# A two-layer transformer block on one core: the last batch's projection first, another batch's down product in TensorE's pause

## The reference

```python
x = layernorm(x + attn0(x))        # 16 heads of 8, softmax over all 256 keys
x = layernorm(x + ffn0(x))         # 128 -> 512, butterflies, gelu, butterflies, 512 -> 128
x = layernorm(x + attn1(x))        # low-rank q and kv, RoPE, causal softmax
x = layernorm(x + ffn1(x))         # silu(x @ wg.T) * (x @ wu.T) @ wd.T, hidden size 384
```

## Time and profile before

| | |
|---|---|
| median of 3 runs | 326.21 us |
| the three runs | 324.72, 326.21, 326.78 us |
| the profiled execution | 325.87 us |
| its span | 324.1 us |
| mean granted TensorE clock | 0.959 |
| busy share of the span: PE, DVE, ACT, POOL | 85%, 78%, 67%, 63% |

### The profile page before, as it was taken

The page is one execution under the profiler, slowest core; times in us unless marked ns, Lnnn a source line. Parts: engine busy times, 40 slices in busy tenths (PEclk is TensorE's granted clock), DMA queues, the critical chain, the costliest instruction groups (busy, mean ns, idle before and its releaser), DMA issues.

```text
span 324.1 us, 9463 instructions
## 1 busy us (share of the span) xinstructions
PE 275.0 (85%) x3194; PEld 200.0 (62%) x3194; DVE 253.7 (78%) x991; ACT 216.5 (67%) x444; POOL 205.3 (63%) x326
## 2 busy tenths in 40 slices
PE   8989969988978999888998896988898787878763
PEld 4766646655565556554676565866676666667553
DVE  4778796886878778897676697598999999775555
ACT  2546883788976799499983999468685757444110
POOL 0529995472448546584779897498879747366332
PEclk9979997999999999999995999899999999899978
DMA  7784350303021130404013140401314040000000
GB/s 228 258 254 144 93 192 15 131 1 131 3 97 35 32 133 17 150 4 155 8 46 120 23 145 11 153 1 41 126 35 148 3 148 20 2 2 18 17 16 32
DMA packets 20495, 25.84 MB, mean 80 GB/s; under 512 B 3744, under 2 KB 14304, under 8 KB 20320
## 3 DMA queue, kind: packets, MB, share of 16 engines
q1 hardware_dynamic: 20016, 24.72, 22.9%
q10 hardware_dynamic: 432, 0.53, 0.4%
HBM read 6.36 MB, written 1.05 MB: 23 GB/s over the span
## 4 chain that ended last, share of the span: by engine, by line
PE 51%; DVE 25%; issue 12%; ACT 9%; POOL 2%; POOLq 0%; ACTq 0%; DVEq 0%
PE bank L632 14%; DVE mx L864 6%; PE bank L388 5%; PE bank L647 4%; DVE room_c L872 4%; ACT E L760 4%; PE bank L398 4%; PE bank L576 4%; PE bank L515 2%; PE bank L597 2%; DVE room_c L898 2%; PE bank L407 2%; PE bank L586 2%; DVE turned L954 2%; PE bank L608 2%
## 5 line engine op out<-in xcount | busy, mean ns | idle before, releaser
L760 ACT ACTIVATE E<-bank 128x512 f32<-128x512 f32 (+1 forms) x256 | 119.7, 549 | 65.4 <-PE bank L411 37.9
L864 DVE TENSOR_REDUCE mx<-bank 128x2 f32<-128x512 f32 x128 | 79.6, 681 | 13.0 <-PE bank L388 12.8
L872 DVE CUSTOM_DVE_ANT_0 room_c<-bank,mask_sb 128x256 f32<-128x256 f32 (+1 forms) x256 | 72.9, 349 | 2.3 <-PE bank L388 2.1
L388 PE MATMUL bank<-QK 32*128 32x256 f32 x480 | 56.0, 308 | 8.4 <-DVE mx L872 3.4
L398 PE MATMUL bank<-QK 32*128 32x256 f32 x480 | 51.8, 311 | 11.5 <-DVE hid L900 6.7
L632 PE MATMUL bank<-E,V 128*32 128x256 f32 (+1 forms) x1024 | 59.5, 376 | 0.2
L388 PEld LDWEIGHTS bank<-QK 32*128 32x128 f32 x480 | 38.4, 187 | 21.4 <-issue 8.9
L1083 POOL TENSOR_SCALAR_AFFINE_SELECT E<-E 128x512 f32<-128x512 f32 x64 | 39.2, 638 | 11.6 <-ACT E L760 11.6
L398 PEld LDWEIGHTS bank<-QK 32*128 32x128 f32 x480 | 35.1, 188 | 17.5 <-DVE hid L900 9.0
L632 PEld LDWEIGHTS bank<-E,V 128*32 128x32 f32 x1024 | 31.0, 115 | 20.7 <-issue 3.6
L954 DVE STREAM_TRANSPOSE turned<-bank 128x256 f32<-128x256 f32 x32 | 14.3, 447 | 21.2 <-PE bank L632 20.9
(11 more groups left out here) (127 smaller groups left out, 561.7 us busy)
## 6 DMA issues: line engine op xcount, KB each, us to landing
spread_qk<-parts SPq DMA_DIRECT2D x30, 256.0 KB, 2.5
spread_qk<-parts SPq DMA_DIRECT2D x60, 128.0 KB, 2.2
room_c<-room_c SPq DMA_DIRECT2D x64, 32.0 KB, 1.9
xb<-x_nat SPq DMA_DIRECT2D x1, 1024.0 KB, 7.1
out<-ln_g SPq DMA_DIRECT2D x7, 128.0 KB, 1.9
xt<-x_t SPq DMA_DIRECT2D x1, 768.0 KB, 7.1
wi<-wi_all SPq DMA_DIRECT2D x1, 576.0 KB, 3.5
room_c<-fac_u SPq DMA_DIRECT2D x1, 508.0 KB, 6.4
```

The lines of the kernel that those rows point to most:

```text
L388: ins = nc.tensor.matmul(g_bank["max", m][:, cols], both[:, 0, c * P:(c + 1) * P], both[:, 1, keys], start=True, stop=True)
L760: act.activation(E[:, a % E_RING, j, 0:n], g_bank["exp", m][:, 0:n], ACT.Exp, scale=SCALE)\
L864: ins = nc.vector.tensor_reduce(mx[:, n % 2, :, i], bank[:, :].rearrange("p (q k) -> p q k", q=QT), AX.X, ALU.max, negate=True)
L872: ins = nc.vector.tensor_tensor_reduce(out=masked_s[:, at % 2, lo:hi], in0=bank[:, lo:hi], in1=mask_sb[:, T + lo - hi:T], scale=-1.0, scal ...
```

## The change

Two entries of `FFN1` move: the down product of batch 13 with its residual and statistics goes from step 264 to 268 (its scaling stays at 272), and the third up chunk of batch 14 from 268 to 264, which moves its tanh too, but not its gate. In TensorE's loop the bodies of transposes and output projection become functions, and for batch 15 alone they are called at another place: the projection ahead of the up chunks of its step, the transposes behind the down product of theirs.

```diff
--- before.py
+++ after.py
@@ -50,8 +50,8 @@
 AT_UP0, AT_GELU, AT_DN0, AT_LN0, AT_XT0 = (52, 52, 56, 56), 60, (64, 68), 72, 76
 
 FFN1 = {b: ((40, 40, 48), 64, 68) for b in range(NB, BATCHES)}
-FFN1.update({BATCHES - 4: ((40, 40, 52), 60, 64), BATCHES - 3: ((40, 44, 52), 56, 64),
-             BATCHES - 2: ((36, 40, 44), 52, 56), BATCHES - 1: ((32, 32, 32), 40, 44)})
+FFN1.update({BATCHES - 4: ((40, 40, 52), 60, 64), BATCHES - 3: ((40, 44, 52), 60, 64),
+             BATCHES - 2: ((36, 40, 40), 52, 56), BATCHES - 1: ((32, 32, 32), 40, 44)})
 
 LATE_GATES = {(BATCHES - 3, 2): HEADS + 4, (BATCHES - 2, 0): HEADS + 8, (BATCHES - 2, 1): HEADS + 12, (BATCHES - 2, 2): HEADS + 12}
 
@@ -524,6 +524,26 @@
                                            wv_sb[:, :] if layer(b) == 0 else wl1[:, 2, :], start=True, stop=True)
                 ins.then_inc(A["v_ps"], 1)
 
+            def turn_tokens(b, g):
+
+                bank = claim(("xt", b), A["xt_ready"], b + 1, g)
+                pe.wait_ge(A["ln_ready"], b + 1)
+                for q in range(QT):
+                    ins = nc.tensor.transpose(bank[:, q * P:(q + 1) * P], NA["ln"][:, b % LN_RING, q, :], id32[:, :])
+                ins.then_inc(A["xt_ps"], 1)
+
+            def project_out(b, g):
+                bank = claim(("proj", b), A["res_done"], b + 1, g)
+                pe.wait_ge(A["att_ready"], b + 1)
+                if b == 0:
+                    pe.wait_ge(ld["bv"], 32)
+                elif b == NB:
+                    pe.wait_ge(ld["next"], 64)
+                for q in range(QT):
+                    ins = nc.tensor.matmul(bank[:, q * P:(q + 1) * P], att[:, q * P:(q + 1) * P],
+                                           (wproj_sb if layer(b) == 0 else wout_sb)[:, :], start=True, stop=True)
+                ins.then_inc(A["proj_ps"], 1)
+
 
             pe.wait_ge(idle_ready, 1)
             for i in range(2):
@@ -554,12 +574,11 @@
                 if (b := projected_at(g)) is not None:
                     semaphore, value = (A["qk_out"], 2 * b) if layer(b) == 0 else (A["y_out"], b - NB + 1)
                     project(b, claim(("qk", b), semaphore, value, g))
-                if (b := turned_at(g)) is not None:
-                    bank = claim(("xt", b), A["xt_ready"], b + 1, g)
-                    pe.wait_ge(A["ln_ready"], b + 1)
-                    for q in range(QT):
-                        ins = nc.tensor.transpose(bank[:, q * P:(q + 1) * P], NA["ln"][:, b % LN_RING, q, :], id32[:, :])
-                    ins.then_inc(A["xt_ps"], 1)
+                if (b := turned_at(g)) is not None and b < BATCHES - 1:
+                    turn_tokens(b, g)
+
+                if attention_at(g, AT_PROJ) == BATCHES - 1:
+                    project_out(BATCHES - 1, g)
                 if (n := tile_at(g, AT_XT0)) is not None:
                     bank = claim(("xt0", n), F0["xt_ready"], n + 1, g)
                     pe.wait_ge(F0["ln_ready"], n + 1)
@@ -597,17 +616,10 @@
                             ins = nc.tensor.matmul(bank[:, q * W:(q + 1) * W], hid1[:, i % 2, c, q * P:(q + 1) * P],
                                                    wf[:, 2, c * W:(c + 1) * W], start=(c == 0), stop=(c == SC - 1))
                     ins.then_inc(F1["down_ps"], 1)
-                if (b := attention_at(g, AT_PROJ)) is not None:
-                    bank = claim(("proj", b), A["res_done"], b + 1, g)
-                    pe.wait_ge(A["att_ready"], b + 1)
-                    if b == 0:
-                        pe.wait_ge(ld["bv"], 32)
-                    elif b == NB:
-                        pe.wait_ge(ld["next"], 64)
-                    for q in range(QT):
-                        ins = nc.tensor.matmul(bank[:, q * P:(q + 1) * P], att[:, q * P:(q + 1) * P],
-                                               (wproj_sb if layer(b) == 0 else wout_sb)[:, :], start=True, stop=True)
-                    ins.then_inc(A["proj_ps"], 1)
+                if turned_at(g) == BATCHES - 1:
+                    turn_tokens(BATCHES - 1, g)
+                if (b := attention_at(g, AT_PROJ)) is not None and b < BATCHES - 1:
+                    project_out(b, g)
                 if (b := values_at(g)) is not None:
                     project_values(b, claim(("v", b), A["v_ready"], b + 1, g))
                 if (n := half_at(g, AT_MT)):
```

## The result

| | before | after |
|---|---|---|
| median of 6 runs each | 325.47 us | 321.97 us |
| lowest and highest | 324.24, 326.94 | 321.04, 326.69 |
| ratio of the times | | 0.988, 95% interval 0.985 to 0.991 |
| span of the profiled execution | 324.1 us | 320.2 us |
| end of `att` of batch 15 | 304.01 us | 304.48 us |

What follows compares the result with a forecast made beforehand. The prediction took the end as bound by batch 15's late projection and TensorE's 3.64 us pause with the low clock after it. Span 324.1 - 4.0 (3.95 + 0.07) = 320.1, plus 2.1 = 322.2 us; range 321.2 to 323.9.

Steps and rivals of the forecast that it cites:

- The projection first: TensorE, batch 15: projection starts at 304.15, right after `att`, and takes 0.61 us; `r_a` starts at 304.80, not 306.98.
- its statistics alone: VectorE: without batch 13 between, `r_a` to `ve_a` takes 1.31 us, not 1.84; `ln_a` starts at 307.12, 2.71 earlier.
- The work moved into the pause: TensorE ahead of transposes 15: up (14, 1), (14, 2) and down 13 fill the wait for `ln_a`, 0.10 us to spare.
- The sum by the Trainium skill: Alternative estimate of the moved TensorE work from the skill's issue gaps: 1.84 us, not 3.14; span 319.9.
- VectorE becomes what sets the end: Behind `ln_a`: residual 13, statistics, five gates 0.86 us apart; last gate ends at 313.51, 3.95 earlier.
- The sum: Whole kernel: 2.71 us gained at `ln_a`, 4.0 at the end; span 320.1 us, plus 2.1 gives 322.2 us.
- The clock rival: TensorE's clock falls at the new pause of about 1.0 us ahead of projection 15; time 323.9 us; chance 0.12.
- Gates that don't run in a row: VectorE behind `ln_a`: three gates each wait about 0.5 us for their tanh; time 323.7 us; chance 0.13.
- The other side: Moved products hold up transposes 15 on TensorE if the low clock lasts some 8 us; time 330.6 us; chance 0.05.
- That it does nothing: Projection 15 can't precede `att` at 304.01, but started 2.2 us behind that, so there is something to gain; no chance given.

Runs made afterwards that it cites:

- tables_only: Kernel before with only the two `FFN1` entries moved, projection and transposes at their old places; ratio to the kernel before 0.999 (0.995 to 1.003).
- no_early_proj: Changed kernel with batch 15's projection back behind up (14, 1) and (14, 2); ratio to the kernel before 0.991 (0.987 to 0.994).
- at_early: Changed kernel with the scaling of batch 12's FFN one step later, so GpSimd multiplies batch 15's `at` first; ratio to the kernel before 0.985 (0.981 to 0.989).
- after_filled: Changed kernel with two unread products of 256 columns added on TensorE ahead of down 13; ratio to the kernel before 0.989 (0.985 to 0.993).
- no_early_filled: Changed kernel with projection 15 back behind the two up chunks, plus three unread products between down 13 and transposes 15; ratio to the kernel before 0.989 (0.983 to 0.994).
- no_late_turn: Changed kernel with batch 15's transposes back ahead of down 13; ratio to the kernel before 0.994 (0.990 to 0.998).
- p_only: Kernel before with only batch 15's projection moved early, tables and transposes as before; ratio to the kernel before 1.004 (1.001 to 1.007).
- before_filled: Kernel before with seven unread products of 256 columns added on TensorE between projection 15 and transposes 15; ratio to the kernel before 0.996 (0.993 to 0.999).
- changed_again: The changed kernel itself, run again beside the others on one chip; ratio to the kernel before 0.990 (0.985 to 0.995).

## Why the prediction was right, point by point

It said 322.2 us, 0.65 for faster; measured were 321.97. All times from the end of `att`:

| step | forecast | measured |
|---|---|---|
| projection 15 | 0.14 | 0.14 |
| `r_a` | 0.79 | 0.86 |
| `ve_a`, `ln_a` | 2.10, 3.11 | 2.18, 3.19 |
| transposes 15 | 3.86 | 3.94 |
| residual 13 | 3.96 | 3.92 |
| up (15, 0) | 4.82 | 4.91 |
| last gate ends | 9.50 | 9.08 |
| residual 15 | 10.82 | 10.46 |
| end of the span | 16.1 | 15.7 |

*The projection first* and *its statistics alone* held. The projection took 0.68 and not 0.61; that is most of the 0.08 which the steps up to the transposes carry. It takes 0.61 right behind other products (before, `tables_only`, `no_early_proj`) and 0.68 where TensorE stood ahead of it, be it for 1.02 us or for 0.15 (`at_early`). *The work moved into the pause*: it filled it, as said. `after_filled` found 0.2 us of spare time where the forecast had 0.10; the down product kept the queue for 1.34 and not 1.41.

*The sum by the Trainium skill* (TensorE: Matmul & The Clock Gate, section Back-to-back issue gap) was 1.84 us for the moved work. The trace has 1.73 for the eight up matmuls (305.30 to 307.03 in the chain) and 1.34 behind them for the down product, 3.1 in all, and two added products of 256 columns cost 0.86, so 0.43 for each. Taken once for each recorded matmul, as the forecast took them, the page's figures do not fit these float32 products: a matmul of 256 columns starts 0.216 after the one before it and not 0.109, one of 128 columns 0.112 ((2.84 - 0.27) / 23, with 0.27 for one alone) and not 0.081. The first is double the figure, the second is not, though the forecast says double of each. Its own terms came from the rows, and they held.

*VectorE becomes what sets the end* is the step with a mis-sized term. The forecast took 0.86 us from gate to gate from 315.72 and 316.58. Without a wait they come 0.76 to 0.79 apart here (309.55, 310.31, then 311.10, 311.89, 312.68). The tanh shows why. ScalarE before:

```profile
316.17 0.38 ACT L790 ACTIVATE th<-bank 128x256 f32<-128x256 f32 x1 [0.48 <-PE bank L586]
```

It ended at 316.55, and the gate started at 316.58: the 0.86 was the pace of TensorE's up chunks (4 x 0.216), handed on by ScalarE, and not VectorE's own. After the change the tanhs still come at that pace,

```profile
311.39 0.39 ACT L802 ACTIVATE th<-bank 128x256 f32<-128x256 f32 x1 [0.48 <-PE bank L605]
312.26 0.38 ACT L802 ACTIVATE th<-bank 128x256 f32<-128x256 f32 x1 [0.48 <-PE bank L605]
```

but the gates have work in stock and go at theirs. The stock is just used up at the last one: its tanh ends at 312.64, and it starts at 312.68. In `no_early_filled`, where they caught up with TensorE, the last three are 0.86 apart again:

```profile
308.61 0.42 DVE L915 SCALAR_TENSOR_TENSOR room_c<-th,bank 128x256 f32<-128x256 f32 x1
...
309.47 0.42 DVE L915 SCALAR_TENSOR_TENSOR room_c<-th,bank 128x256 f32<-128x256 f32 x1
...
310.33 0.42 DVE L915 SCALAR_TENSOR_TENSOR room_c<-th,bank 128x256 f32<-128x256 f32 x1
```

So four intervals that are 0.31 shorter in all and a start 0.11 earlier make the last gate 0.42 earlier. But 0.06 of it is lost at once: residual 15 comes 1.38 behind the end of the last gate and not 1.32, since down 14 and 15 run in one piece from 312.06 to 314.90. The forecast had TensorE 0.5 us ahead of VectorE at the last gate, and residual 14 right behind it. TensorE is not ahead: residual 14 comes just behind down 14, whose twelve matmuls end at an estimated 313.56 (312.06 + 11 x 0.112 + 0.27). In the changed kernel it starts 0.47 after the start of the last `hid` (313.13 to 313.60). In `no_late_turn`, where down 14 had been done, it took 0.34:

```profile
314.08 0.42 DVE L910 TENSOR_TENSOR hid<-bank,room_c 128x256 f32<-128x256 f32 x1
314.42 0.41 DVE L945 TENSOR_TENSOR r_g<-bank,ln_a 128x256 f32<-128x256 f32 x1
```

So from up (15, 0) on it is TensorE that sets the end of the changed kernel, with 2.67 us to the start of down 14, 2.84 for the two down products and 0.04 to residual 15. That VectorE would set it was wrong, if by 0.1 us only: its gates run faster than the forecast had them, and TensorE is next in line.

*The sum* has the span right at 320.1 against 320.2, and that closeness is luck, with two misses that cancel: the rest was 0.37 shorter than forecast, and `att` ended 0.47 later than in the profile of before. The 0.34 that the forecast added for a median above the profiled run did not come again either (321.97 and 321.96). The gain of the rest was 4.4 us for 4.0 forecast. That `att` would still end at 304.01 was too simple: with no change to what it waits for it ended between 301.7 (`no_early_filled`) and 309.3 (`p_only`), with the clock low at other places ahead of it.

*The clock rival* did not come. The pause of 1.02 stood in the changed kernel twice, in `no_late_turn`, `after_filled` and `p_only`, and in none of them did a fall follow closely; in `p_only` it came six microseconds later, in the long pause. *Gates that don't run in a row*: of the kernels with the new tables only `no_early_proj` has gates behind `ln_a` that wait for their tanh, with the low clock (0.77 and 0.83; 0.61 and 0.83 in its second profile). *The other side* had the right mechanism, as `after_filled` shows by its size, and too little of it: 0.2 us to spare, and no low clock. *That it does nothing* is nearly what the early projection alone and the tables alone do: 0.1 us more and 0.4 us less of rest than before.

The forecast had 1.3 us behind `ln_a`, as the low clock that no longer comes less the VectorE work that now lies there, and did not split the two. The runs do: 1.7 us of the 4.4 are the clock. The forecast's 2.71 for `ln_a` was 2.63 (5.82 to 3.19). From the start of `ln_a` to the end `before_filled` takes 12.60 us and the changed kernel 12.53, so with the clock held the stretch behind `ln_a` takes nearly the same time in both orders, with more work for VectorE in the changed kernel and less for TensorE.

## What to carry to other kernels

A step has to be moved on every engine that it passes: in `p_only` the projection moved on TensorE alone ran 2.2 us earlier and its residual stood behind another batch's on VectorE, later than before. Work of other batches belongs into the wait that the last batch makes anyway, behind its own critical product and ahead of the next one, and its length has to fit: 0.86 us too much cost 0.76. What such work saves can also be the clock, 1.7 us here, and products whose result nobody reads show how much of it. And a period read between two instructions may be the pace of whoever feeds them; see whether the second one found its input there or had just got it.

## What the runs showed of the hardware that had not been expected

The clock fell after shorter pauses than the 3.64 us of the kernel before: it was at 0.50 from some 2 us behind the end of a pause of 1.77 us in both profiles of `no_early_proj`'s kernel (a second pause, of 0.56, lay between). In `no_early_filled`, with 0.48 in place of the 1.77, it did not fall. It did not fall behind pauses of 1.02 and 1.39 us in `no_late_turn`. At the end of the kernel before it stayed low for 3.4 us, at the end of `tables_only` for 6.7 (307.0 to 313.7). And it fell at different places in executions of the same instructions: at 281 to 284 us in the profile of before, at 263 to 267 in the one of after, at 222 to 225 and 256 to 259 in `changed_again`. One execution of `tables_only`, of which there is no profile, took 420.93 us with a mean granted clock of 0.56. `att` moved by microseconds along with the low stretches, and I take the one for the cause of the other, and of most of the spread between executions; that was argued from the traces and not tested by itself.
